# At most two scatters of the slot list in flight: a wait on one of two semaphores before each scatter

## The chip, the core and the metric

The kernel runs on one core of a Trainium2 chip. The metric is the device time of one execution in microseconds (us). Three runs of the kernel before took 1495.07, 1495.42 and 1499.51 us, so the median is 1495.42 us. The profile was taken in one execution, whose span from the first to the last instruction is 1494.3 us.

## The reference

The input is x, 2 sequences of 4096 tokens with 256 features, 8192 tokens in all. One layer is computed:

```
xn = layernorm(x)                                        # per token
s  = attention(xn)      # 16 heads of 16, 12 sampled positions per query:
     q, k, v = xn@wq.T+bq, xn@wk.T+bk, xn@wv.T+bv
     off = tanh(pw_w @ gelu(depthwise_conv3(q)) + pw_b) * 6
     positions = clip(token + linspace(-2, 2, 12) + off, 0, 4095)
     sk, sv = k, v interpolated linearly at positions
     attn = softmax(q.sk / 4 - rel_scale*|positions - token|)
     s = (sum attn*sv) @ wo.T + bo
g  = silu(mixture_of_experts(xn))   # 8 experts of hidden 512, the best 2 per token:
     scores = xn@Wr.T + br ; top 2 of scores + biases_N ; their softmax weights, renormalised
     y = sum over the 2 chosen experts e of w_e * ((silu(a_e)*b_e) @ Wl2[e] + bl2[e])
     with a_e, b_e = the halves of xn@Wl1[e] + bl1[e]
out = x + s * g
```

## The kernel before

The program has two blocks, and between them all engines meet at a barrier, so nothing of the second block starts before every engine has ended the first.

**The first block** (`front_block`) works in 16 steps of 512 tokens (`STEPS`, `GROUP` = 4 tiles of 128 tokens). It normalises x, computes v and the router's scores, then q and k, and then for each step the products of the queries with the slopes of the keys (`head_scores`, L638; ScalarE copies them out in L514, and SyncE stores them in `S_rows`, L335), the convolution (L756 to L764), the offsets (L650, L770) and the sampled positions (`positions`, L783 to L788, stored in L340). Early in this block VectorE also routes the tokens: it chooses two experts for each token and gives each of the 16384 pairs of token and choice a place in a list sorted by expert. The places are ready at L851 (`list_row`, semaphore `list_rows`).

**The slot list.** The list lies in memory off the chip (`slot_list`, 18176 entries of 4 bytes, filled beforehand with numbers of spare rows, L421). GpSimd writes the token numbers into it by 128 indirect DMAs, here called scatters (L430, `LISTED` = 128). Each takes one column of `list_row` as its addresses and one column of `token_i` as its data: 128 partitions, one number of 4 bytes each. All 128 add 16 to the same semaphore, `scattered`, as they land, and GpSimd waits only once, for 16 * 128, ahead of the load of the finished list (L450). So it issues a scatter as soon as it has issued the one before.

Among the scatters GpSimd also issues four DMAs that clear the accumulator of the expert outputs (`clear_moe`, L438, 2 MB each: after 32, 64, 96 and 120 scatters), and after the last scatter three small clears (L445 to L447). All of these DMAs go through one queue, q0, the one of GpSimd's DMAs. SyncE's are on q1.

**After the list.** VectorE waits for the loaded list at L924 and turns it into row numbers (L925, L926, tile `inv`, named token_of in the trace). This wait stands late in VectorE's own order: behind it come only the positions of the last step (L783 to L788), which SyncE then stores (L340). SyncE waits for the landing of all stores (L387 to L394), and the block ends.

**The second block** (`mix_block`) gathers the rows of xn by the list (L1156), runs the experts on 71 pairs of 128 slots (PE L1446, L1452) and adds the results back by indirect DMAs (L1175). Beside that VectorE computes the attention weights of 16 steps (L1603, L1643, L1647). At the end the weights are applied to v, projected, multiplied by the gates and stored. GpSimd's first instruction in this block is the gather L1156 by the list.

Of the kernel before, what the change touches and what calls it, by code (L numbers as in the profile page):

```python
# [64 lines left out]
LISTED = TOPK * TILES  # L65
COUNT_AT = 1
OPEN_AT = 6
ROWS_AHEAD = 4
BAND_SLOTS = 4
MOE_SLOTS = 8  # L70
# [75 lines left out]
def front_block(nc, io, dram, keep):  # L146


    with ExitStack() as ctx:
        def sb(name, shape, dt=F32):  # L150
            return ctx.enter_context(nc.sbuf_tensor(name, shape, dt))
# [4 lines left out]
        def sem(name):  # L156
            return ctx.enter_context(nc.semaphore(name))
# [53 lines left out]
        token_i = sb("token_i", [P, TOPK * TILES], I32)  # L211
# [37 lines left out]
        consts = sem("consts")  # L249
        x_loaded = [sem(f"x_loaded{u}") for u in range(ROWS_AHEAD)]  # L250
        xn_ready = sem("xn_ready")
# [35 lines left out]
        prefix_ready = sem("prefix_ready")  # L287
        list_set = sem("list_set")
        list_rows = sem("list_rows")
        scattered = sem("scattered")  # L290
        list_loaded = sem("list_loaded")

        TAIL = VROWS - TOKENS - REACH
# [15 lines left out]
        def x_in(n):  # L309
            return x_slots[n % ROWS_AHEAD].rearrange("p (a c) -> p a c", a=GROUP)  # L310

        def rows_of(n):
            return slice(n * GTOK, (n + 1) * GTOK)
# [4 lines left out]
        def _(sp):  # L318
            def load_x(n):
                sp.dma_start(x_in(n), io["x"][rows_of(n), :].rearrange("(a p) c -> p a c", p=P)).then_inc(  # L320
                    x_loaded[n % ROWS_AHEAD], 16)

            def store_xn(n):
                sp.wait_ge(xn_ready, n + 1)
                sp.dma_start(dram["xn"][rows_of(n), 0:D].rearrange("(a p) c -> p a c", p=P), xn[:, n % 2]).then_inc(
                    xn_stored[n % 2], 16)
# [11 lines left out]
            def store_pos(n):  # L338
                sp.wait_ge(pos_ready, n + 1)
                sp.dma_start(dram["pos"][rows_of(n), :].rearrange("(a p) c -> p a c", p=P), pos[:, n % 2]).then_inc(  # L340
                    pos_stored[n % 2], 16)

            def load_opening():

                sp.wait_ge(list_rows, 1)
                for u in range(SX_SLOTS):
                    sp.wait_ge(sx_stored[u], 16)
                sp.wait_ge(pos_stored[0], 16)
                for to, rows in keep["slopes_in"](0):
                    sp.dma_start(to, rows).then_inc(keep["s_loaded"], 16)  # L350
                for at, loaded in ((keep["posn"], keep["posn_loaded"]), (keep["posw"], keep["pos_loaded"])):
                    sp.dma_start(at.rearrange("p (a c) -> p a c", a=GROUP),
                                 dram["pos"][rows_of(0), :].rearrange("(a p) c -> p a c", p=P)).then_inc(loaded, 16)
# [8 lines left out]
            for n in range(STEPS):  # L362
                store_xn(n)
                if n + ROWS_AHEAD < STEPS:
                    load_x(n + ROWS_AHEAD)
                if n > 0:
# [11 lines left out]
            for n in range(STEPS):  # L378
                for a in range(GROUP):
                    store_s(n, a)  # L380
                    if a == 1 and n >= 2:
                        store_pos(n - 2)
                if n == OPEN_AT:
                    load_opening()
# [11 lines left out]
        @block.gpsimd  # L396
        def _(pool):
            nc.gpsimd.memset(zeros[:], 0.0).then_inc(zeros_set, 1)
            nc.gpsimd.memset(keep["ident"][:], 0.0).then_inc(zeros_set, 1)
            pool.wait_ge(zeros_set, 2)  # L400
            nc.gpsimd.affine_select(out=keep["ident"][:], in_=keep["ident"][:], compare_op=ALU.not_equal, fill=1.0,
                                    base=0, pattern=[[-1, P]], channel_multiplier=1).then_inc(zeros_set, 1)

            for row, rows in ((0, REACH), (REACH + TOKENS, TAIL)):
                pool.dma_start(dram["v"][row:row + rows, :], zeros[0:rows, :]).then_inc(pads_set, 16)
            nc.gpsimd.memset(ones[:], 1.0).then_inc(consts, 1)
            pool.wait_ge(consts, 1)

            nc.gpsimd.affine_select(out=below[:], in_=ones[:], compare_op=ALU.is_gt, fill=0.0, base=0,
                                    pattern=[[1, P]], channel_multiplier=-1).then_inc(consts, 1)  # L410
            nc.gpsimd.iota(rows_i[:], pattern=[[-1, EXPERTS]], base=EXPERTS, channel_multiplier=0).then_inc(consts, 1)
            nc.gpsimd.iota(base_i[:], pattern=[[P, SEQ // P]], base=0, channel_multiplier=1).then_inc(consts, 1)
            nc.gpsimd.iota(keep["tile_exp"][:], pattern=[[PAIR, SLOT_PAIRS]], base=0, channel_multiplier=0).then_inc(consts, 1)

            nc.gpsimd.iota(head_i[:], pattern=[[0, 1]], base=0, channel_multiplier=1).then_inc(consts, 1)
            nc.gpsimd.iota(spare_i[:].rearrange("p (n s) -> p n s", s=2), pattern=[[0, HIGH // 2], [P, 2]], base=0,
                           channel_multiplier=1).then_inc(consts, 1)
            nc.gpsimd.iota(token_i[:].rearrange("p (k t) -> p k t", k=TOPK), pattern=[[0, TOPK], [P, TILES]], base=-TOKENS,
                           channel_multiplier=1).then_inc(consts, 1)
            pool.wait_ge(consts, CONSTS)  # L420
            pool.dma_start(dram["list"].rearrange("(p n) o -> p (n o)", p=P), spare_i[:]).then_inc(list_set, 16)  # L421
            pool.wait_ge(gates_ready, 1)
            for q in range(4):
                some = slice(q * TILES // 4, (q + 1) * TILES // 4)
                pool.dma_start(dram["xn"][0:TOKENS].rearrange("(t p) c -> p t c", p=P)[:, some, D:], scores[:, some]).then_inc(gates_stored, 16)
            pool.wait_ge(list_set, 16)
            pool.wait_ge(list_rows, 1)
            def scatter(some):
                for c in some:
                    nc.gpsimd.indirect_dma_start(  # L430
                        out=dram["list"], out_offset=bass.IndirectOffsetOnAxis(ap=list_row[:, c:c + 1], axis=0),
                        in_=token_i[:, c:c + 1], in_offset=None).then_inc(scattered, 16)

            def clear_moe(q):

                pool.wait_ge(pos_ready, 3 * q + 3)
                some = slice(q * TILES // 4, (q + 1) * TILES // 4)
                pool.dma_start(dram["moe"][0:TOKENS].rearrange("(t p) c -> p t c", p=P)[:, some],  # L438
                               zeros[:, None, :].broadcast_to([P, TILES // 4, D])).then_inc(pads_set, 16)

            for q in range(4):
                scatter(range(q * LISTED // 4, min((q + 1) * LISTED // 4, LISTED - 8)))
                clear_moe(q)
            scatter(range(LISTED - 8, LISTED))
            pool.dma_start(dram["moe"][TOKENS:, :].rearrange("(s p) c -> p s c", p=P), zeros[:, None, :].broadcast_to([P, 2, D])).then_inc(pads_set, 16)  # L445
            pool.dma_start(dram["xn"][TOKENS:, 0:D].rearrange("(s p) c -> p s c", p=P), zeros[:, None, :].broadcast_to([P, 2, D])).then_inc(pads_set, 16)
            pool.dma_start(dram["xn"][TOKENS:, D:].rearrange("(s p) c -> p s c", p=P),  # L447
                           zeros[:, None, 0:EXPERTS].broadcast_to([P, 2, EXPERTS])).then_inc(pads_set, 16)
            pool.wait_ge(scattered, 16 * LISTED)
            pool.dma_start(spare_i[:], dram["list"].rearrange("(p n) o -> p (n o)", p=P)).then_inc(list_loaded, 16)  # L450
            pool.wait_ge(gates_stored, 16 * 4)

# [246 lines left out]
        def _(dve):  # L699
# [10 lines left out]
            def moments(n):  # L710
                u = n % 2
                dve.wait_ge(x_loaded[n % ROWS_AHEAD], 16 * (n // ROWS_AHEAD) + 16)
                for a in range(GROUP):
# [1024 lines left out]
def build(nc, io):  # L1738
# [10 lines left out]
    with ExitStack() as ctx:  # L1749
# [24 lines left out]
        with nc.sbuf_tensor("scores", [P, TILES, EXPERTS], F32) as scores, \  # L1774
                nc.sbuf_tensor("qT", [P, KC, BATCH * (SEQ + 2)], F32) as qT, \
                nc.sbuf_tensor("kT", [P, KC, TOKENS + 1 + 2 * REACH], F32) as kT:
            keep.update(scores=scores, qT=qT, kT=kT)
            front_block(nc, io, dram, keep)
# [38 lines left out]
```

## Time and profile before

| what | value |
|---|---|
| three runs: median (lowest to highest) | 1495.42 us (1495.07 to 1499.51) |
| the profiled execution: its span | 1494.3 us |
| its time beyond the span, by the median of the runs | 1.1 us |
| first block, to the barrier | 0 to 362.9 us |
| scatters of the slot list (L430) | issued from 163.6 to 339.9 us |
| second block | 362.9 to 1494.3 us |
| busy share of the span | PE 91%, VectorE 86%, ScalarE 55%, GpSimd 54% |

An engine's busy share is an average over both blocks. In the rows below, a line of the timeline gives the start, the length and the engine of an instruction or of a run of like ones, then the idle time of that engine before it and what ended it. "issue" means that nothing the profile shows was waited for. DMAs are counted on the engine that issues them, for as long as the issuing takes. When the data has landed is told by the views of landings, and by the waits.

### The profile page before, as it was taken

To read this page: it belongs to the slowest core of one execution; us is meant where nothing else is said; L and a number is where in the kernel's file an instruction comes from. 1 tells how busy PE (TensorE), PEld (TensorE's weight loads), DVE (VectorE), ACT (ScalarE), POOL (GpSimd) and SP (SyncE) were. 2 spreads that over 40 slices of the span, in tenths; PEclk is the share of its full clock that TensorE was granted. 3 is DMA by queue.
4 is the path that set the end of the run, shared out by engine and by line. 5 is a ranking of instruction groups with operands and counts; after the bars stand their busy time and mean duration, and the time that the engine had idled before them with its cause. 6 is when DMAs were issued, how large, how long until landed. Compare 5 with 4: busy or idle time off the path is not lost.

```text
span 1494.3 us, 35841 instructions
## 1 busy us (share of the span) xinstructions
PE 1361.6 (91%) x13687; PEld 1085.4 (73%) x13688; DVE 1280.2 (86%) x1504; ACT 823.8 (55%) x1889; POOL 804.3 (54%) x566
## 2 busy tenths in 40 slices
PE   5998899984799999999999998999999978797988
PEld 4864565653688888888888886887888856675766
DVE  7837655556699999999999999999999999999961
ACT  2547687864445555555555554554555436574655
POOL 1001477773587766767666877768686651311111
PEclk9999999985999999999999999999999988898999
DMA  7933366564957676768677666767777679999897
GB/s 231 352 130 101 115 203 208 166 222 158 287 122 224 170 232 161 222 161 235 183 204 214 168 179 160 214 159 201 196 190 221 133 178 232 250 218 246 217 246 148
DMA packets 203481, 293.52 MB, mean 196 GB/s; under 512 B 24833, under 2 KB 160261, under 8 KB 203123
## 3 DMA queue, kind: packets, MB, share of 16 engines
q0 software_dynamic: 65792, 146.59, 38.5%
q1 hardware_dynamic: 134915, 144.84, 33.6%
q8 instruction: 52, 0.85, 0.3%
q10 hardware_dynamic: 2672, 0.83, 0.2%
q14 instruction: 50, 0.41, 0.1%
HBM read 182.83 MB, written 117.74 MB: 201 GB/s over the span
## 4 chain that ended last, share of the span: by engine, by line
DVE 48%; DMA 8%; PE 8%; issue 6%; SPq 5%; POOL 0%; ACT 0%; POOLq 0%; DVEq 0%
DVE gslope L1647 11%; DVE parts L1643 11%; DVE parts L1603 8%; DMA band<-band_rows 7%; DVE expert_mem L1569 5%; PE pB L1480 3%; DVE parts L1615 3%; SPq L1121 2%; DVE parts L1619 2%; DVE parts L1622 1%; PE pA L1465 1%; PE pY L1490 1%; DVE gslope L1700 1%; SPq L1115 1%; DVE wgt L1708 1%
## 5 line engine op out<-in xcount | busy, mean ns | idle before, releaser
L1175 POOL DMA_INDIRECT moe_rows<-expert_mem,token_of x142 | 324.9, 2288 | 76.2 <-issue 47.9
L1446 PE MATMUL pA<-xsT,expert_mem 128*128 128x256 f32 x1136 | 264.5, 387 | 22.6 <-DMA expert_mem<-in_w_l 15.5
L1156 POOL DMA_INDIRECT expert_mem<-xn_rows,token_of x142 | 222.3, 1566 | 96.8 <-issue 74.2
L1452 PE MATMUL pY<-expert_mem 128*128 x1136 | 265.7, 387 | 0.0
L1446 PEld LDWEIGHTS pA<-xsT,expert_mem 128*128 128x128 f32 x1136 | 220.3, 195 | 55.9 <-issue 20.0
L1446 PE MATMUL pB<-xsT,expert_mem 128*128 128x256 f32 x1136 | 256.8, 379 | 0.0
L1452 PEld LDWEIGHTS pY<-expert_mem 128*128 128x128 f32 x1136 | 211.1, 191 | 42.3 <-issue 16.2
L1446 PEld LDWEIGHTS pB<-xsT,expert_mem 128*128 128x128 f32 x1136 | 215.8, 190 | 29.3
L1643 DVE SCALAR_TENSOR_TENSOR parts<-pos_pair,prob 128x768 f32<-128x768 f32 x256 | 228.0, 953 | 1.1
L1647 DVE TENSOR_REDUCE gslope<-parts 128x256 f32<-128x3072 f32 x64 | 214.7, 3354 | 2.2
L1297 ACT ACTIVATE expert_mem<-pA,b1sel 128x256 f32<-128x256 f32 x284 | 111.3, 474 | 135.3 <-issue 93.2
L1603 DVE SCALAR_TENSOR_TENSOR parts<-posT,bend 128x768 f32<-128x768 f32 x192 | 168.9, 952 | 4.1 <-ACT posT L1358 4.1
L430 POOL DMA_INDIRECT slot_list<-token_i,high_part x128 | 132.8, 1037 | 56.9 <-issue 38.7
L1306 ACT ACTIVATE expert_mem<-pB,b1sel 128x256 f32<-128x256 f32 x284 | 111.6, 477 | 92.8 <-PE pB L1446 92.8
L1315 ACT ACTIVATE expert_mem<-pY,gsel 128x256 f32<-128x256 f32 x142 | 59.7, 472 | 157.1 <-PE pY L1452 157.1
L1165 POOL DMA_DIRECT2D expert_mem<-in_w_l x71 | 68.2, 961 | 103.7 <-PE pX L1440 64.9
L618 PE MATMUL pQK<-qT,wqk 128*128 128x512 f32 x256 | 122.9, 625 | 1.0 <-ACT qT L492 0.8
L1214 POOL DMA_DIRECT2D out<-expert_mem x15 | 19.4, 1295 | 188.1 <-DVE expert_mem L1654 171.2
L1615 DVE TENSOR_TENSOR parts<-parts 128x5376 f32<-128x5376 f32 x16 | 92.2, 5763 | 0.6
L1569 DVE TENSOR_TENSOR expert_mem<-expert_mem 128x1024 f32<-128x1024 f32 x71 | 87.0, 1226 | 6.2 <-ACT expert_mem L1306 2.8
L638 PEld LDWEIGHTS pS<-kT,qm 32*64 32x64 f32 x4096 | 56.1, 139 | 45.1 <-issue 42.1
L618 PEld LDWEIGHTS pQK<-qT,wqk 128*128 128x128 f32 x256 | 48.0, 197 | 53.8 <-issue 50.2
(197 smaller groups left out, 2036.3 us busy)
## 6 DMA issues: line engine op xcount, KB each, us to landing
expert_mem<-in_w_l POOLq DMA_DIRECT2D x71, 1024.0 KB, 7.0
band<-band_rows SPq DMA_DIRECT2D x256, 96.0 KB, 5.5
S_rows<-stage SPq DMA_DIRECT2D x64, 376.0 KB
band_rows<-wgt SPq DMA_DIRECT2D x12, 1536.0 KB, 7.1
pos_pair<-pos_rows SPq DMA_DIRECT2D x28, 384.0 KB, 7.7
xn_rows<-stage SPq DMA_DIRECT2D x16, 512.0 KB, 5.4
v_rows<-stage SPq DMA_DIRECT2D x16, 512.0 KB, 4.2
moe_rows<-zeros POOLq DMA_DIRECT2D x4, 2048.0 KB
```

What stands on the lines that cost most here:

```text
L430: nc.gpsimd.indirect_dma_start(out=dram["list"], out_offset=bass.IndirectOffsetOnAxis(ap=list_row[:, c:c + 1], axis=0), in_=token_i[:, c:c ...
L618: mm = nc.tensor.matmul(pQK[:, c], wqk[:, k, first:first + P], qT[:, k, qcol(m):qcol(m) + GTOK], start=(k == 0), stop=(k == KC - 1))
L1156: nc.gpsimd.indirect_dma_start(out=xs[:, u, s], out_offset=None, in_=dram["xn"], in_offset=bass.IndirectOffsetOnAxis(ap=keep["inv"][:, 2 * ...
L1175: nc.gpsimd.indirect_dma_start(out=dram["moe"], out_offset=bass.IndirectOffsetOnAxis(ap=keep["inv"][:, 2 * n + s:2 * n + s + 1], axis=0), ...
L1306: ins = nc.scalar.activation(hid[:, h, c], pB[:, c], ACT.Identity, bias=b1sel[:, u, HC + c:HC + c + 1])
L1446: mm = nc.tensor.matmul(dst[:, c], w1[:, 1 - u, k, o * HID + c * P:o * HID + (c + 1) * P], xsT[:, k], start=(k == 0), stop=(k == KC - 1))
L1452: mm = nc.tensor.matmul(pY[:, s], hid[:, h, c, s * P:(s + 1) * P], w2[:, c, ds(e * D, D)], start=False, stop=(s == 1 and c == HC - 1))
L1569: V.tensor_tensor(hid[:, h], hid[:, h], act_a[:, h % 2], ALU.mult).then_inc(hid_ready, 1)
L1603: ins = V.scalar_tensor_tensor(in_block(parts[:, i]), in_block(posT[:].rearrange("p b q -> p (b q)")), float(i + 1 - REACH), each_in_block ...
L1615: chain.count(V.tensor_tensor(parts[:, 0:7], parts[:, 0:7], parts[:, 7:14], ALU.add))
L1643: ins = V.scalar_tensor_tensor(terms[:, i], at, float(j - REACH), prob[:], ALU.max, ALU.mult)
L1647: chain(V.tensor_reduce(G[:, :, batch * BATCHED:(batch + 1) * BATCHED].rearrange("p t j -> p j t"), terms.rearrange("p j (t r) -> p j t r" ...
```

## The change

Instead of one semaphore there are two. Scatter number c adds 16 to `scattered[c % 2]` as it lands. Ahead of scatter c, from c = 2 on, GpSimd waits until scatter c - 2, which has the same semaphore, has landed. So no more than two are in flight, and a semaphore is counted by one scatter at a time. Ahead of the load of the list GpSimd waits for both semaphores, 16 * 64 each. The order of the DMAs is as before.

```
-        scattered = sem("scattered")
+        scattered = [sem(f"scattered{u}") for u in range(SCATTERS_OPEN)]      # SCATTERS_OPEN = 2
...
             def scatter(some):
                 for c in some:
+                    if c >= SCATTERS_OPEN:
+                        pool.wait_ge(scattered[c % SCATTERS_OPEN], 16 * (c // SCATTERS_OPEN))
                     nc.gpsimd.indirect_dma_start(
                         out=dram["list"], out_offset=bass.IndirectOffsetOnAxis(ap=list_row[:, c:c + 1], axis=0),
-                        in_=token_i[:, c:c + 1], in_offset=None).then_inc(scattered, 16)
+                        in_=token_i[:, c:c + 1], in_offset=None).then_inc(scattered[c % SCATTERS_OPEN], 16)
...
-            pool.wait_ge(scattered, 16 * LISTED)
+            for u in range(SCATTERS_OPEN):
+                pool.wait_ge(scattered[u], 16 * (LISTED // SCATTERS_OPEN))
```

On GpSimd, the end of the row of DMAs before, from the third group of scatters to the end of the block (L430 is a scatter, L438 a clear of 2 MB, L450 the load of the list):

```order
L430 DMA slot_list<-token_i,high_part 18176x1 x32
L438 DMA moe_rows<-zeros 128x16x256 [waits pos_ready]
L430 DMA slot_list<-token_i,high_part 18176x1 x24
L438 DMA moe_rows<-zeros 128x16x256 [waits pos_ready]
L430 DMA slot_list<-token_i,high_part 18176x1 x8
L445 DMA moe_rows<-zeros 128x2x256
L446 DMA xn_rows<-zeros 128x2x256
L447 DMA xn_rows<-zeros 128x2x8
L450 DMA spare_i<-slot_list 128x142 [waits scattered]
```

Now, around the fourth clear (the lines are three or four further down in the changed file: L433, L441, L454), and behind the eighth scatter after it:

```order
L433 DMA slot_list<-token_i,high_part 18176x1 [waits scattered0]
L433 DMA slot_list<-token_i,high_part 18176x1 [waits scattered1]
L441 DMA moe_rows<-zeros 128x16x256 [waits pos_ready]
L433 DMA slot_list<-token_i,high_part 18176x1 [waits scattered0]
L433 DMA slot_list<-token_i,high_part 18176x1 [waits scattered1]
...
L448 DMA moe_rows<-zeros 128x2x256
L449 DMA xn_rows<-zeros 128x2x256
L450 DMA xn_rows<-zeros 128x2x8
L454 DMA spare_i<-slot_list 128x142 [waits scattered1,scattered0]
```

No instruction has moved. Each scatter but the first two now carries a wait of its own, in turn on the two semaphores, and the clears stand unchanged between them. On the other engines the rows are the same as before.

## Rows read from the trace of the kernel before

**Rows 1.** Page, part 1 and the first lines of part 2.

```profile
PE 1361.6 (91%) x13687; PEld 1085.4 (73%) x13688; DVE 1280.2 (86%) x1504; ACT 823.8 (55%) x1889; POOL 804.3 (54%) x566
POOL 1001477773587766767666877768686651311111
```

**Rows 2.** Page, part 5, the scatters: busy us, mean ns | idle before.

```profile
L430 POOL DMA_INDIRECT slot_list<-token_i,high_part x128 | 132.8, 1037 | 56.9 <-issue 38.7
```

**Rows 3.** Timeline of POOL, 150 to 500 us: start us, us, engine line op.

```profile
163.57 1.05 POOL L430 DMA_INDIRECT slot_list<-token_i,high_part  x1 [18.14 <-DVE high_part L851]
174.88 0.97 POOL L430 DMA_INDIRECT slot_list<-token_i,high_part  x1 [0.30 <-issue]
176.15 0.97 POOL L430 DMA_INDIRECT slot_list<-token_i,high_part  x1 [0.30 <-issue]
...
251.39 1.20 POOL L438 DMA_DIRECT2D moe_rows<-zeros  x1
...
338.93 0.97 POOL L430 DMA_INDIRECT slot_list<-token_i,high_part  x1 [0.30 <-issue]
...
341.39 0.74 POOL L447 DMA_DIRECT2D xn_rows<-zeros  x1
342.69 0.78 POOL L450 DMA_DIRECT2D spare_i<-slot_list  x1 [0.56 <-DMA slot_list<-token_i,high_part]
363.68 1.68 POOL L1156 DMA_INDIRECT expert_mem<-xn_rows,token_of  x1 [20.20 <-POOLq L149]
```

**Rows 4.** DMA issues by line: KB, median us to landing.

```profile
spare_i<-slot_list POOLq DMA_DIRECT2D x1, 71.0 KB, 4.0
```

**Rows 5.** Timeline of DVE, 325 to 372 us.

```profile
355.87 0.55 DVE L770 TENSOR_TENSOR off<-pOff,pw_b 128x384 f32<-128x384 f32 x1
356.34 0.23 DVE L925 CAST list_f<-spare_i 128x142 f32<-128x142 int32 x1
356.60 0.24 DVE L926 TENSOR_SCALAR token_of<-list_f 128x142 uint32<-128x142 f32 x1
357.33 0.96 DVE L783 SCALAR_TENSOR_TENSOR pos<-off,pos 128x768 f32<-128x768 f32 x1 [0.49 <-ACT off L535]
358.33 0.26 DVE L786 TENSOR_SCALAR pos<-pos 128x192 f32<-128x192 f32 x1
358.62 1.00 DVE L788 TENSOR_SCALAR pos<-pos,base 128x192 f32<-128x192 f32 x4
363.07 0.17 DVE L1564 MEMSET ones<- 3x128 bf16 x1 [3.45 <-PEq L149]
```

**Rows 6.** Waits of the SP queue, 343 to 372 us: us, times, longest.

```profile
SPq L392 <- DMA pos_rows<-pos: 2.2, 1, 2.2
```

**Rows 7.** The gathers of line L1156, whole trace: duration ns, landing us.

```profile
L1156 POOL DMA_INDIRECT expert_mem<-xn_rows,token_of x142: 945/1290/10487, 363.7 to 1170.3; - x142
DMA to landing us min/median/max: 2.8/4.8/13.8
```

**Rows 8.** DMA queues (packets, MB, share) in 251:260, 260:261 and 261:262.

```profile
q0 software_dynamic: 530, 1.91, 63.2%
q0 software_dynamic: 131, 0.17, 59.2%
q0 software_dynamic: 35, 0.02, 8.1%
```

**Rows 9.** The same view for 165 to 206 us, between start and first clear.

```profile
q1 hardware_dynamic: 4576, 5.42, 38.0%
q0 software_dynamic: 967, 0.02, 1.8%
```

**Rows 10.** Stretches: busy us of each engine, PEclk, DMA share, GB/s.

```profile
330.00:343.00 13.00, 9.56 (x207) 8.64 (x208) 3.54 (x9) 6.84 (x14) 10.30 (x12) 0.50 0.81 266
...
357.00:369.00 12.00, 0.00 (x0) 0.00 (x0) 7.85 (x15) 4.51 (x10) 4.71 (x4) 0.59 0.28 90
369.00:376.00 7.00, 4.14 (x11) 3.23 (x12) 6.96 (x9) 0.91 (x3) 6.69 (x5) 0.50 0.92 305
```

More of the change, by code:

```diff
@@ L67 @@
 OPEN_AT = 6
+SCATTERS_OPEN = 2
 ROWS_AHEAD = 4
```

## The prediction, made before the changed kernel was run

> **What bounds the kernel now.** I read the page first, then GpSimd's timeline around the scatters, then what ends the first block, then every landing that can stand in for a scatter's. The page shows PE and VectorE busy for most of the span and GpSimd for half of it, but GpSimd is at seven tenths of each slice just while it issues the scatters [rows 1]. Averages say nothing here: what counts is the barrier at 362.9 us, before which nothing of the second block starts. GpSimd's first gather comes 0.8 us behind it [rows 3].
>
> The reader is to see three things. First, the scatters run at GpSimd's own pace. They start 1.27 us apart (174.88, 176.15), 0.97 us of issuing and 0.30 us of "issue" [rows 3]; over all 128 the mean is (132.8 + 38.7) / 128 = 1.34 us, since some issues last up to 1.5 us [rows 2]; of the 56.9 us idle, 18.1 are the first one's wait for its addresses [rows 3]. They never wait for a landing. Second, the list is early: its load is issued at 342.69 and lands 4.0 us later, at 346.7 [rows 3, 4], but VectorE comes to it only at 356.34, straight out of its own work [rows 5]. So there are 9.6 us of slack, and the first block ends by the positions and their store, not by the list. Third, the tail behind the list: L925 starts at 356.34, the positions end at 359.6, SyncE waits 2.2 us for the last store, and the barrier opens at 362.9 [rows 5, 6]. That tail is 6.5 us, of which 0.5 us is a wait for ScalarE that will be over if the list is late.
>
> **What the change removes and moves.** Nothing is removed, and the order of the DMAs stays. 126 scatters gain a wait for the landing of the scatter two places ahead. Queued behind each wait on GpSimd are the next scatters, the four clears, the load of the list, and through it VectorE (L925), SyncE's last store and the barrier. So GpSimd's pace becomes two scatters in one time from issue to landing, here called a round, if that is longer than 2 x 1.34 = 2.7 us.
>
> **How long a round is.** The trace gives no landing for a scatter, but one is bracketed. The last starts at 338.93; GpSimd ends its next three DMAs at 341.39 + 0.74 = 342.13 and then still waits for a scatter, to 342.69 [rows 3]. From issue to the start of the waiting instruction is thus at least 3.2 and at most 3.76 us. The nearest likeness, the gathers of L1156, land after 2.8 us at the least and 4.8 in the median, but among much other traffic and often behind a 1 MB load [rows 7]. I take 3.5 us, inside the bracket. Bounds: 2.8 (the shortest gather, nothing for the reaction) and 5.0 (the median gather and 0.2). The scatters themselves load the queue with next to nothing, 1.8% [rows 9], so what lasts is latency, and it goes on whether SyncE's stores run (38% on q1) or have ended. 64 rounds of 3.5 us are 224 us.
>
> The Trainium skill, "DMA: Bandwidth & Descriptors", section "Anatomy of one DMA", gives every DMA of GpSimd a fixed cost of about 2.0 us, which an estimate by that page would make a round shorter than GpSimd's own pace, so that the waits would cost nothing by themselves. The bracket of at least 3.2 us contradicts it, if that cost is counted from the issue.
>
> **The clears.** The clear issued at 251.39 has moved its 2.1 MB by about 261.3: 1.91 + 0.17 MB before 261, 0.02 after it [rows 8]. That is 9.9 us from issue in q0, the queue in which the scatters stand too. Before, GpSimd went on issuing behind it and lost nothing. Now two more scatters are issued, and then it waits until the first of them has landed. In a round that starts at 0, the second scatter is issued by 2.3 us and then the clear; the queue is free at 12.2, the scatter behind lands 2.3 us later (3.5 less its issue and 0.2) and GpSimd goes on at 14.7, where it would have gone on at 7.0. That is 7.7 us for each of the four, 31 us in all. Bounds: nothing, if a scatter's landing does not depend on the clear ahead of it, and 8.3 us each with a round of 2.8 us.
>
> **The sum.** First scatter 163.6; + 224 + 31 + 1.3 (the second scatter of the last round comes that much later) = 419.9, the issue of the list's load, 77 us later than before. Landed at 423.9. VectorE's L925 goes from 356.3 to 423.9, +67.6: the first 9.6 us of the delay cost nothing because VectorE's own work covers them, the rest is on the path. Less the 0.5 us wait for ScalarE: the barrier opens 67 us later. Every wait and load of the second block hangs on the barrier, so I move it whole. The pause of PE gets longer, but its clock stood at 0.50, the lower level of 1.2 GHz, already in 330 to 343 us, and again in the first 7 us of its work in the second block after 12 us without a matmul [rows 10]; it starts cold both times, so I put nothing for it (bounds 0 and 3 us). No other engine gains: the scatters took only 1.8% of the queues' time. The profiled span becomes 1494.3 + 67 = 1561.3; with the 1.1 us by which the median of the runs lies above it, 1562.5.
>
> With both low bounds of the round (2.8) and full clears the list is 25 us late behind its slack, 1520; with 3.5 and no cost of the clears, 1532; with 5.0 throughout, 1652.
>
> **Rivals.**
>
> A. Landings are slow while SyncE stores. Until 357 us there is q1 at 38% [rows 9], and the median gather among traffic took 4.8 us [rows 7]. With rounds of 5.0 us and two clears at 6.2 us, 36 rounds are done by 357; 28 rounds of 3.5 and two clears of 7.7 remain, 113 us. The load goes out at 471.7, the barrier 119 us later: 1614. For it: the bracket was taken at a single place. Against it: that place had a clear and three stores beside it. The same page of the Trainium skill, section "Queues, rings and completion order", says that a DMA's semaphore count lands only after every earlier write of that DMA engine, across its queues, which would speak for A; no row here separates it.
>
> B. Rounds are about as short as the shortest gather, or the clears hold nothing back: 1520 to 1532. For it: 2.8 us was seen [rows 7]. Against it: 3.2 us was exceeded here, and scatter and clear stand in one queue.
>
> C. A scatter lands within two issues, 2.7 us; the waits are met on arrival and only the clears stall, four times about 7.5 us. The load goes out at 372.7, VectorE is 20 us late: 1515. Only the 0.56 us wait [rows 3] speaks against it, and that may be the reaction to a semaphore already full.
>
> D. Not slower: the semaphores fill at GpSimd's pace whatever stands ahead in the queue, clears too. Then all waits are met on arrival and the list comes as before; it may come up to 9.6 us later without any effect, and beyond that each microsecond costs one. 1495. That is also the case of a change that does not limit anything.
>
> **How the numbers follow.** Forecast (1540 to 1590) 50%, A 20%, B 17%, C 9%, D 4%. The range takes in the forecast, B, part of C and A up to 1625: 1518 to 1625. Within 0.3% (about what a measurement of this kernel can tell from no change, 4.5 us) only D ends, 3%; faster 1%, for something in D that I don't see; slower 96%.
>
> **What would show it.** In the changed profile the idle time before the scatters is put down to the landing of a scatter, not to "issue"; it is about 64 x (3.5 - 2.7) and four waits of some 8 us behind the clears. Scatters come in pairs 3.5 us apart. The load of the list goes out near 420, VectorE has one wait for it of some 60 us, PE and ScalarE are idle from about 357 to 430, and the second block lasts 1131 us as before. Pairs 5 us apart before 357 and closer after it would be A; no waits behind the clears, B; pairs 2.7 us apart, C; a barrier at 363, D. The prediction is wrong if the pace before 357 and after it differ much, or if the second block changes its length.

## The result, and the profile after

The changed kernel takes 1563.08 us in the median of 4 runs (1549.46 to 1566.25). The kernel before takes 1495.24. The ratio is 1.0426, with a 95% interval of 1.0381 to 1.047: slower by 68 us. The forecast was 1562.5. The sum came out, but its main term, one length of a round for all scatters, was too short for the first part of them and too long for the rest, and the two errors cancelled, so the total says less than it seems. Some later executions count as slow ones, over 1.5% above the fastest of their kernel (two of about 2660 us, of the kernel before and of the one with eight in flight, and five of the ten of the first run with the clears early), and every ratio is taken from the fast ones alone.

The page of the changed kernel, part 1, answers to [rows 1]. The engines' busy times have hardly changed (PE 1361.6 to 1358.5 us), only their shares of a longer span.

```profile
span 1560.8 us, 35842 instructions
PE 1358.5 (87%) x13687; PEld 1082.2 (69%) x13688; DVE 1279.0 (82%) x1504; ACT 823.2 (53%) x1889; POOL 814.7 (52%) x566
```

The scatters in part 5 of that page answer to [rows 2]. They are as long as before (132.3 us), but the idle time before them has grown from 56.9 to 133.0 us, and 88.5 us of it is now put down to the landing of an earlier scatter.

```profile
L433 POOL DMA_INDIRECT slot_list<-token_i,high_part x128 | 132.3, 1033 | 133.0 <-DMA slot_list<-token_i,high_part 88.5
```

GpSimd's timeline in the changed kernel answers to [rows 3]: start us, us, engine line, and in brackets the idle time and what ended it.

```profile
168.44 1.05 POOL L433 DMA_INDIRECT slot_list<-token_i,high_part  x1 [19.25 <-DVE high_part L855]
...
179.69 0.97 POOL L433 DMA_INDIRECT slot_list<-token_i,high_part  x1 [1.41 <-DMA slot_list<-token_i,high_part]
181.00 0.97 POOL L433 DMA_INDIRECT slot_list<-token_i,high_part  x1 [0.34 <-DMA slot_list<-token_i,high_part]
184.07 1.08 POOL L433 DMA_INDIRECT slot_list<-token_i,high_part  x1 [2.10 <-DMA slot_list<-token_i,high_part]
...
242.22 1.68 POOL L433 DMA_INDIRECT slot_list<-token_i,high_part  x1 [7.97 <-DMA slot_list<-token_i,high_part]
...
303.55 1.20 POOL L441 DMA_DIRECT2D moe_rows<-zeros  x1
305.06 1.01 POOL L433 DMA_INDIRECT slot_list<-token_i,high_part  x1 [0.30 <-issue]
306.37 1.73 POOL L433 DMA_INDIRECT slot_list<-token_i,high_part  x1 [0.31 <-issue]
316.16 0.97 POOL L433 DMA_INDIRECT slot_list<-token_i,high_part  x1 [8.06 <-DMA slot_list<-token_i,high_part]
...
365.83 1.20 POOL L441 DMA_DIRECT2D moe_rows<-zeros  x1
367.34 1.00 POOL L433 DMA_INDIRECT slot_list<-token_i,high_part  x1 [0.30 <-issue]
368.64 0.97 POOL L433 DMA_INDIRECT slot_list<-token_i,high_part  x1 [0.30 <-issue]
374.99 0.97 POOL L433 DMA_INDIRECT slot_list<-token_i,high_part  x1 [5.38 <-DMA slot_list<-token_i,high_part]
376.26 0.97 POOL L433 DMA_INDIRECT slot_list<-token_i,high_part  x1 [0.31 <-issue]
377.54 0.97 POOL L433 DMA_INDIRECT slot_list<-token_i,high_part  x1 [0.30 <-issue]
...
411.95 0.97 POOL L433 DMA_INDIRECT slot_list<-token_i,high_part  x1 [5.38 <-DMA slot_list<-token_i,high_part]
...
421.51 0.61 POOL L454 DMA_DIRECT2D spare_i<-slot_list  x1
```

The reader is to see three kinds of time. To 352 us, while the other engines work, nearly every second scatter has a wait, of 0.3 to 2.9 us (40 waits, 60.9 us, for 86 scatters); their starts are 1.97 us apart in the mean, so a round of two is 3.94 us. From 355 us on the other engines have ended and the 42 scatters left are 1.28 us apart, GpSimd's own pace: each wait is met on arrival. And behind each clear there is one long wait: 8.0 and 8.1 us in the first part, 5.4 and 5.4 us in the second.

VectorE's end of the first block answers to [rows 5]. It came to the list at 351.8 and had to wait for it for 72 us.

```profile
351.26 0.54 DVE L774 TENSOR_TENSOR off<-pOff,pw_b 128x384 f32<-128x384 f32 x1
423.76 0.24 DVE L929 CAST list_f<-spare_i 128x142 f32<-128x142 int32 x1 [71.95 <-DMA spare_i<-slot_list]
...
425.46 1.01 DVE L792 TENSOR_SCALAR pos<-pos,base 128x192 f32<-128x192 f32 x4
429.92 0.17 DVE L1568 MEMSET ones<- 3x128 bf16 x1 [3.46 <-PEq L150]
```

Stretches of the changed kernel (busy us of each engine, then PEclk, DMA share, GB/s) answer to [rows 10]. From 352 to 430 us PE, VectorE and ScalarE do next to nothing, at the lower clock level. The stretch behind it, the second block, is as long as it was: 1130.8 us here, 1131.3 before.

```profile
352.00:430.00 78.00, 0.00 (x0) 0.00 (x0) 2.68 (x9) 0.83 (x2) 46.92 (x49) 0.51 0.23 73
...
430.00:1560.80 1130.80, 1048.53 (x8691) 870.62 (x8691) 1056.67 (x893) 597.46 (x1452) 665.73 (x408) 0.96 0.77 199
```

### The profile page after: what moved, and what is told of

Its sections match the earlier page's. It is cut to its first block and busy times, and to the rows that moved or that the text cites. A ratio compares the mean times of both kernels' runs of the same rounds, so it can differ in the third digit from the quotient of the medians.

```text
span 1560.8 us, 35842 instructions
## 1 busy us (share of the span) xinstructions
PE 1358.5 (87%) x13687; PEld 1082.2 (69%) x13688; DVE 1279.0 (82%) x1504; ACT 823.2 (53%) x1889; POOL 814.7 (52%) x566
## 5 line engine op out<-in xcount | busy, mean ns | idle before, releaser
L1179 POOL DMA_INDIRECT moe_rows<-expert_mem,token_of x142 | 339.6, 2391 | 75.9 <-issue 47.1
L1160 POOL DMA_INDIRECT expert_mem<-xn_rows,token_of x142 | 218.5, 1539 | 91.0 <-issue 80.7
L433 POOL DMA_INDIRECT slot_list<-token_i,high_part x128 | 132.3, 1033 | 133.0 <-DMA slot_list<-token_i,high_part 88.5
L1444 PE MATMUL pX<-ident,expert_mem 128*128 128x128 f32 x284 | 43.1, 275 | 85.5 <-DMA expert_mem<-xn_rows,token_of 85.5
L1444 PEld LDWEIGHTS pX<-ident,expert_mem 128*128 128x128 f32 x284 | 35.7, 142 | 92.9 <-DMA expert_mem<-xn_rows,token_of 85.8
```

What stands on the lines that cost most here:

```text
L433: nc.gpsimd.indirect_dma_start(out=dram["list"], out_offset=bass.IndirectOffsetOnAxis(ap=list_row[:, c:c + 1], axis=0), in_=token_i[:, c:c ...
L1160: nc.gpsimd.indirect_dma_start(out=xs[:, u, s], out_offset=None, in_=dram["xn"], in_offset=bass.IndirectOffsetOnAxis(ap=keep["inv"][:, 2 * ...
L1179: nc.gpsimd.indirect_dma_start(out=dram["moe"], out_offset=bass.IndirectOffsetOnAxis(ap=keep["inv"][:, 2 * n + s:2 * n + s + 1], axis=0), ...
```

## The experiments

Where nothing else is said, a kernel is the changed one with one more edit, and the intervals are from the start of a scatter to the start of the next. The runs were made on several chips. On one of them the kernel before takes 1646 to 1649 us in the median, not 1495; the last section is on that. It is called the chip of 1649 here, and a time on it can only be read against that number.

### One in flight

```
-SCATTERS_OPEN = 2
+SCATTERS_OPEN = 1
```

> One scatter in flight instead of two, so that each start-to-start interval is one whole time from issue to landing. Theory T (a landing is slow only beside SyncE's stores): intervals of 3.5 to 4 us until the stores end near 352 us, 2.3 to 2.5 us after that, about 1715 us in all. Rival U (the landing takes the same 3.5 us with or without the stores, as the prediction had it, and the fast pace late in the changed kernel has another cause): 3.5 us throughout, about 1495 + 128 x 3.5 - 171 + 30 - 10 = 1790 us.

Measured: 1712.2 us, on the chip of 1649. With one in flight each interval is a landing, and GpSimd's timeline shows it directly, first beside the block's own work, then in the quiet part:

```profile
208.76 0.97 POOL L433 DMA_INDIRECT slot_list<-token_i,high_part  x1 [4.47 <-DMA slot_list<-token_i,high_part]
212.99 0.97 POOL L433 DMA_INDIRECT slot_list<-token_i,high_part  x1 [3.26 <-DMA slot_list<-token_i,high_part]
215.40 1.14 POOL L433 DMA_INDIRECT slot_list<-token_i,high_part  x1 [1.44 <-DMA slot_list<-token_i,high_part]
...
411.33 0.97 POOL L433 DMA_INDIRECT slot_list<-token_i,high_part  x1 [1.43 <-DMA slot_list<-token_i,high_part]
413.73 0.97 POOL L433 DMA_INDIRECT slot_list<-token_i,high_part  x1 [1.43 <-DMA slot_list<-token_i,high_part]
```

To 352 us the intervals are 2.39 to 7.09 us, 3.84 in the mean, without the two at the first clear. From 372 us on, after the work has ended, they are 2.40 us, one like the other, save at the clears and one of 3.4. So an undisturbed landing is 2.40 us from the issue, less than two issues of 1.28 us; beside the work it is three of them in the mean. Theory T's numbers held in the mean, though not its cause, as will be seen; the uniform 3.5 us of rival U did not.

### Four and eight in flight

```
-SCATTERS_OPEN = 2
+SCATTERS_OPEN = 4      # and 8
```

> Four in flight. Theory T: four issues take 5.1 to 5.4 us, more than most landings beside the stores (3.5 to 4), so the scatters keep GpSimd's own pace; only the four clears still stall, by 12.2 + 0.2 - 1.2 - 5.1 = 5 to 6 us beside the stores. The list's load goes out some 23 us later than before, 9.6 of them slack: about 1508 us. Rival V (landings beside the stores often take over 5 us, so four are too few as well): waits in ordinary places too, and over 1520 us.

> Eight in flight. Theory T: eight issues and the clear's own take 11.4 us, and a scatter behind a clear lands after 12.2 us, so that under 2 us is left of each clear's stall, under 8 in all, inside the slack of 9.6 us: 1495 us, the same as before. Rival W (each wait costs something by itself, or a semaphore is slow to be seen): 120 waits of 0.1 to 0.3 us, 12 to 36 us, of which the slack takes 9.6: 1498 to 1522 us.

> Eight in flight, again for a chip where before takes 1495 us. Landings were 2.4 us with nothing beside them and 3.9 us in the mean, 7 at most, beside the first block's own work, so eight issues of 1.28 us cover every one but those behind a clear, where under 2 us is left of each stall: the list is 5 to 8 us later, inside the slack of 9.6: 1495 us. Rival (each of the 120 waits costs something by itself): 1500 to 1520.

Measured: four, 1639.93 us, a ratio to the kernel before of 0.994 (0.9911 to 0.9968); eight, 1652.08 us, 1.0013 (0.9993 to 1.0032). Both were on the chip of 1649, where neither expectation can be tested. Eight in flight was run again on a chip where the kernel before takes 1497.38: 1497.61 us, a ratio of 0.9996 (0.9975 to 1.0017). In its waits GpSimd waited for no scatter at all:

```profile
POOL slot_list L433 <- issue: 38.7, 127, 0.3
...
POOL slot_list L433 <- DVE high_part L855: 19.3, 1, 19.3
```

That is the same 38.7 us of "issue" as before [rows 2]: 120 waits that are met cost nothing. So the whole loss comes from waits that are not met. No wait is left behind a clear either: the scatter that waits for the one right behind a clear starts 10.5 to 11.2 us after it at GpSimd's own pace, and in the changed kernel such a scatter had landed after 11.1 us (305.06 to 316.16), in the quiet part after 7.7 (367.34 to 374.99). Four in flight was not run where the kernel before takes 1495.

### The clears ahead of the scatters

```
-                clear_moe(q)
...
+            pool.wait_ge(r_ready, STEPS)              # once the scores of all tokens are there
+            for q in range(4):
+                pool.dma_start(dram["moe"][...][:, some], zeros[...]).then_inc(pads_set, 16)
             pool.wait_ge(gates_ready, 1)
```

> Two in flight as in the changed kernel, but the four clears are issued before the scatters, once the scores of all tokens are there (near 110 us). Theory T with the clears' stalls as read from the changed profile (8.0 and 8.1 us beside the stores, 5.4 and 5.4 after them, and 1.2 us of issuing each): the scatters go on by 18 us in the time of the stores, which is worth 11 us of scatters later, and 13 us of clears later are gone: 24 to 25 us less than the changed kernel, about 1538 us. Rival X (the time behind a clear is caught up elsewhere, so that it costs nothing): as the changed kernel, 1563 us.

> The clears ahead of the scatters, two in flight, as in the run of the same kernel whose chip gave 1649 us for the kernel before and hid the effect. Where before takes 1495: theory (scatter and clear stand in one queue; stalls of 8.0, 8.1, 5.4 and 5.4 us and 1.2 us of issuing each, as read from the changed kernel's profile) 24 to 25 us less than the changed kernel, 1538. Rival (what a clear costs is caught up elsewhere): 1563.

Measured: the first run, on the chip of 1649, gave 1632 to 1668 us, a ratio of 0.9985 (0.9943 to 1.0027), and tells nothing of the clears. The second, beside a kernel before of 1497.38, 1551.16 us, a ratio of 1.0352 (1.0314 to 1.0391). That is 12 us less than the changed kernel and half of what was expected. The waits before the scatters beside the work, from 166 to 352 us:

```profile
POOL slot_list L438 <- DMA slot_list<-token_i,high_part: 76.9, 39, 3.6
```

No wait of over 5 us stands before a scatter any more, and the two in the quiet part are gone: with two issues of 1.2 us they are 13.2 us, about all that was gained. The sum beside the work is what the changed kernel has there with its two long waits (60.9 and 16.0 us); only it is now spread over ordinary waits, 0.87 us for each of 88 scatters instead of 0.71. So by this profile the clears' stalls beside the work were caught up elsewhere: the theory was right for the quiet clears, the rival for the others. Why the ordinary waits grew was not found, and it is one profile; a second one of the changed kernel (the next experiment) has 0.69 us for each.

### The changed kernel once more, and the list at another address

```
     dram = {
+        "list": nc.dram_tensor("slot_list", [SLOTS, 1], I32).ap(),     # in the kernel before, not the changed one
...
-        "list": nc.dram_tensor("slot_list", [SLOTS, 1], I32).ap(),
```

> The changed kernel itself once more, two in flight. On the chip of the last four runs the kernel before took 1649 us, 154 more than where the change was timed, all of it in the first block: while the scatters run at GpSimd's full pace there, PE issues its matmuls many times slower. If this is such a chip: theory S (what slows PE is the pace of the scatters) expects the waits of two in flight to slow the scatters only while SyncE stores, and each stall of PE to stop the stores and so the waits, so that the time is near the kernel before's, 1630 to 1660; rival (the waits alone decide, as where the change was timed): before + 67 us. If the kernel before takes 1495 us here: 1563 by both.

> The kernel before, all scatters in flight, with only the slot list declared ahead of the other arrays in the memory off the chip, so that it lies at another address. Theory M (on the chip where before takes 1649 the small writes hit a part of memory that PE's instructions come from): the time changes by over 20 us there. Rival (the place of the list plays no part): the same as before, whichever of the two times before has here.

Measured, with a kernel before of 1498.42 us: the changed kernel 1563.98 us, a ratio of 1.0444 (1.0424 to 1.0464), the same loss again, with 6.2, 6.6, 5.4 and 5.4 us of waiting behind the clears in its profile; the kernel before with the list declared first, 1497.51 us, 1.0002 (0.9976 to 1.0028). The second had been meant for the chip of 1649 and did not come to it, so theory M was not tried.

### SyncE's stores made small, or turned into loads

```
-                sp.dma_start(bass.AP(dram["S"].tensor, ..., [[S_ROW, P], ...]), Sx[:, a])
+                sp.dma_start(bass.AP(dram["S"].tensor, ..., [[S_ROW, 1], ...]), Sx[0:1, a])       # e5: 3 KB
+                sp.dma_start(Sx[:, a], bass.AP(io["x"].tensor, ..., [[S_ROW, P], ...]))           # e6: a load
```

> Two in flight, but SyncE's stores of the slope products write 3 KB instead of 376 KB each, and the second block takes these numbers from x, so part of the result is not computed. Theory T (landings are slow only beside the stores): scatters at GpSimd's own pace of 1.27 us from the start, save beside the 384 KB stores of positions, one in 14 us; the clears stall 5.4 us each as they did after the stores; the load of the list goes out 20 to 25 us after where the kernel before has it, and the whole is about 1508 where before takes 1495. Rival Y (landings are slow beside the work of PE, VectorE and ScalarE, which ends at the same time as the stores): rounds of 3.9 us as in the changed kernel, 1563.

> Two in flight, and SyncE's 376 KB stores are turned into loads of the same shape from x into the same tile (the second block takes its numbers from x, so part of the result is not computed). Theory T1 (any traffic of that size on the 16 DMA engines slows the landings): mean start-to-start intervals of 1.9 to 2.0 us as in the changed kernel, 1560 where before takes 1495. Rival T2 (what slows them is writing to the memory off the chip, whose confirmations a scatter's semaphore waits for): intervals near 1.3 us, 1508 to 1515.

Measured, one run of each beside a kernel before of 1498.42: 1549.94 us with the small stores, 1571.28 us with the loads. The waits before the scatters, of both (us, times, longest), the small stores first:

```profile
POOL slot_list L434 <- DMA slot_list<-token_i,high_part: 63.1, 34, 6.0
```

```profile
POOL slot_list L433 <- DMA slot_list<-token_i,high_part: 97.2, 48, 7.3
```

In the changed kernel it was 88.5 us in 46. Less the long waits behind the clears, and counted only beside the block's own work, it is 0.71 us for a scatter in the changed kernel, 0.40 with the small stores and 0.89 with the loads. So theory T falls as it was put: without the stores' bytes (q1's share of the DMA engines falls from 42% to 11%) more than half of the waiting remains. The bytes have a part in it, and loads hold the landings up no less than stores, which T1 had right.

### Added work beside single scatters

One scatter in flight, and in the quiet part, before each engine's wait for the list, work of one kind after the other; for PE's small matmuls for instance:

```
+            for i in range(24):
+                ...                                    # the 64 small matmuls of head_scores
+                mm.then_inc(phase[2], 1)
+                pe.wait_ge(phase[2], i + 1)
```

> One scatter in flight, so that each start-to-start interval is a landing, and in the quiet stretch after the first block's own work, where an interval was 2.40 us, work is added that the result does not need, one kind after the other: VectorE (20 operations of 128x1024 from two tiles, 26 us), PE (56 matmuls of 128x512, 28 us), PE (24 times the 64 small matmuls of the slope products, 30 us), ScalarE (36 activations of 128x512, 29 us), SyncE (40 stores of 3 KB, 25 us), SyncE (10 stores of 376 KB, one at a time, 35 us). With the stores cut to 3 KB the scatters still waited, so the theory that only SyncE's bytes slow a landing has fallen. Theory Y1 (PE's instructions, which come from the memory off the chip): intervals of 3 us and more in the two stretches of PE, most with the small matmuls, 2.4 elsewhere. Y2 (VectorE, which keeps GpSimd from writing its descriptors): over 3 us in the first stretch alone. Y3 (the number of SyncE's DMAs): in the stretch of 3 KB stores. Y4 (ScalarE): in its stretch. Y5 (the bytes after all): only in the last. If each stretch stays near 2.4 but the last, the slowing needs several engines at once.

Measured: 1727.75 us, on the chip of 1649; what counts are the intervals in each stretch. GpSimd's timeline, two rows from each: VectorE's operations, PE's small matmuls, ScalarE's activations, the 3 KB stores, the 376 KB stores.

```profile
389.34 1.09 POOL L443 DMA_INDIRECT slot_list<-token_i,high_part  x1 [1.43 <-DMA slot_list<-token_i,high_part]
391.87 1.08 POOL L443 DMA_INDIRECT slot_list<-token_i,high_part  x1 [1.44 <-DMA slot_list<-token_i,high_part]
...
467.48 0.97 POOL L443 DMA_INDIRECT slot_list<-token_i,high_part  x1 [3.00 <-DMA slot_list<-token_i,high_part]
471.42 0.97 POOL L443 DMA_INDIRECT slot_list<-token_i,high_part  x1 [2.97 <-DMA slot_list<-token_i,high_part]
...
512.58 0.97 POOL L443 DMA_INDIRECT slot_list<-token_i,high_part  x1 [1.44 <-DMA slot_list<-token_i,high_part]
514.98 0.97 POOL L443 DMA_INDIRECT slot_list<-token_i,high_part  x1 [1.43 <-DMA slot_list<-token_i,high_part]
...
527.00 0.97 POOL L443 DMA_INDIRECT slot_list<-token_i,high_part  x1 [1.44 <-DMA slot_list<-token_i,high_part]
529.39 0.97 POOL L443 DMA_INDIRECT slot_list<-token_i,high_part  x1 [1.43 <-DMA slot_list<-token_i,high_part]
...
541.39 0.97 POOL L443 DMA_INDIRECT slot_list<-token_i,high_part  x1 [1.43 <-DMA slot_list<-token_i,high_part]
543.79 0.97 POOL L443 DMA_INDIRECT slot_list<-token_i,high_part  x1 [1.43 <-DMA slot_list<-token_i,high_part]
```

The intervals are 2.5 us beside VectorE (the issue itself is 0.1 longer, the wait for the landing is not; the first three, 3.0 to 3.3 us, follow close on the block's own last stores), 2.40 beside PE's large matmuls and ScalarE, 2.40 beside both kinds of stores but for single ones of up to 2.6. Only beside PE's small matmuls, from 457 to 497 us, they are 3.3 to 4.1 us. Of the kinds taken alone, theory Y1 is the one that holds, and for the small matmuls only. In that stretch the queue of instructions moved more than in the 54 us of large matmuls before it (packets, MB, share of 16 engines; 457 to 497 us, then 400 to 454):

```profile
q8 instruction: 10, 0.16, 1.8%
```

```profile
q8 instruction: 2, 0.03, 0.2%
```

10 packets of 16 KB in 40 us, with 1344 weight loads and as many matmuls in it: small matmuls use up instructions fast, and these come over the same 16 DMA engines. The Trainium skill, "Runtime: NRT & Kernel Launch", section "Instruction fetch mechanics", says that each engine refills its instructions in blocks of 16 KiB, 256 instructions; the 2688 of this stretch would be 10.5 blocks, and the row agrees with 10.

Is it these packets that hold a landing up, or the matmuls? The same view has the GB/s of each microsecond from 457 to 497 us, and a packet stands out in it as 16 or 17:

```profile
GB/s 0 1 0 16 1 0 0 16 1 0 0 16 1 0 0 17 0 0 0 1 16 0 0 17 0 0 0 17 0 0 16 1 0 0 16 1 0 0 17 0
```

The packets start at 460, 464, 468, 472, 477 us and so on, one in each of the long intervals (their scatters start at 460.25, 463.52, 467.48, 471.42 and 475.20). The first block's traces bear it out, when the scatters are sorted by whether a packet of an instruction queue (q8, or q14 with its 8 KB) starts within 2.4 us of a scatter's issue, those near a clear left out. With one in flight the intervals are 4.55 us with such a packet (24 of them) and 3.05 without (21). With the small stores the scatter two places on waits 0.78 us with it (43) and 0.08 without (41). There PE's small matmuls can be told from the packets: where they fill a third or more of those 2.4 us, the wait is 0.82 us with a packet (26) and 0.10 without (22). So it goes with the packets, not with the matmuls. In the changed kernel it is 1.04 against 0.45 us, and with the loads, where q1 has 50%, no difference is seen (0.96 and 1.04). No edit moved the packets alone, and one packet, at 453.5 us beside the large matmuls, held nothing up.

### Few small matmuls in the first block

```
                         for g in range(RG):
+                            if N >= 12 and (c, s, g) != (KC - 1, SUBS - 1, RG - 1):
+                                continue
```

> Two in flight as in the changed kernel, but from the 13th tile on PE issues 1 of the 64 small matmuls of the slope products (3276 of 4096 are left out, so part of the result is not computed); ScalarE copies out and SyncE stores as before. With one scatter in flight the small matmuls were the one kind of added work beside which landings rose, from 2.4 to 3.3 to 4.1 us. Theory Y1 (they lengthen the landings in the first block too): start-to-start intervals of 1.3 to 1.5 us in the mean between the clears, where the changed kernel had 1.98, few waits, the list's load 40 us earlier or more. Rival (something else in the first block, as its stores and its other work together): intervals of 1.8 to 2.0 us.

Measured: 1545.91 us beside a kernel before of 1492.54. GpSimd's group in part 5 of its page:

```profile
L433 POOL DMA_INDIRECT slot_list<-token_i,high_part x128 | 129.9, 1015 | 113.7 <-DMA slot_list<-token_i,high_part 66.1
```

66.1 us of waiting where the changed kernel had 88.5. Beside the work, and without the waits behind clears, it is 41 us for 91 scatters, 0.45 us each instead of 0.71. The load of the list goes out at 400.1, 21 us earlier, half of what Y1 expected. So Y1 explains a good third of the waiting, as the bytes of the stores do, and neither is the whole cause. It is one run of each, and leaving out matmuls left out the instruction packets too: 4 of 16 KB between 168 and 340 us instead of 28.

## Why the prediction came out

**The slack and the tail: right.** The list was late by 67.4 us at VectorE (356.3 to 423.8, forecast 423.9), and the barrier by 67, as the 9.6 us of slack and the unchanged tail demanded. Three small shifts met in it: the scatters began 4.9 us later than before, which the other profiles of these kernels also do by 2 to 5 us, the way from the first scatter to the list's load was 3 us shorter than forecast (253 against 256), and the load of the list landed in 2.2 us instead of the 4.0 of [rows 4]. Eight in flight, with its list load issued at 346.85 and VectorE at it at 356.97 without a wait, shows the slack too.

**The second block: right.** It moved whole, 1131.3 to 1130.8 us, and the longer pause of PE cost nothing.

**The round of 3.5 us throughout: the step that failed.** The prediction had said that what lasts is latency, and that "it goes on whether SyncE's stores run (38% on q1) or have ended". It does not. Beside the first block's work a round was 3.94 us, and after it the landing of 2.40 us is below the two issues of 2.55, so that GpSimd's own pace holds. The bracket of 3.2 to 3.76 us was taken at a place where the engines still worked and a clear had just been moved, and I used it for the quiet part as well. A pace that differs much before 357 us and after it was the prediction's own sign of being wrong, and it came. Rival A had the dependence on the other work right, with 5.0 us too long a round; rival C, the waits met on arrival, is what the quiet part showed. The sum over both parts came out by luck: 86 scatters at 1.97 us and 42 at 1.28 are 223 us, and the 128 at 1.75 that had been put down are 224.

The page "DMA: Bandwidth & Descriptors" of the Trainium skill, section "Anatomy of one DMA", with its fixed cost of about 2.0 us, fits the quiet landing here, 2.40 us from the start of the issue and 1.43 from its end. I had set it aside on the strength of a bracket that other work had stretched. The same page's rule in "Queues, rings and completion order", that a DMA engine's count lands only after its every earlier write, across its queues, was not borne out by the one test of stores alone: beside 376 KB stores issued one at a time the landings stayed at 2.40 us, one of 2.58 apart. In the first block, where the bytes of the stores did count, no run separates this rule from the mere sharing of the engines.

**The clears: the mechanism right, two of four too dear.** Forecast 7.7 us each, 31 in all; measured 8.0, 8.1, 5.4 and 5.4, 26.8 in all. In the changed kernel's second profile they are 6.2, 6.6, 5.4 and 5.4. The two cheap ones ran with no other traffic beside them. Moved ahead of the scatters they gave back 12 us, not 27, which is the two quiet ones with their issues; those beside the work were caught up elsewhere.

**D, not slower: excluded** by the two timings, 1.0426 and 1.0444.

**What stays open.** Taking away the bytes or the small matmuls leaves 0.40 to 0.45 us of waiting for a scatter; both together were not taken away. Without the bytes almost all that is left stands beside an instruction packet (0.78 us against 0.08), so little else seems to be needed in that kernel; but that is read from a trace and not tried. And why the bytes lengthen a landing in the first block, when the same stores alone did not, was not found.

## What to carry to other kernels

A limit on DMAs in flight costs nothing as long as the number in flight times the issue pace covers the landing; here eight times 1.28 us was enough and two was not. The landing to put in is the one beside the real work (here 3.8 us in the mean, up to 7), not a quiet one (2.4), and right behind a large DMA in the same queue it is longer still (behind 2 MB 7.7 us in the quiet part and 11 to 12 beside the work). A landing read at one place of a trace holds for the work beside that place: look for stretches of the kernel where that work differs before using it for all.

## What was not expected of the hardware

**Scatters at full pace can starve PE, on one chip.** On one chip the kernel before takes 1649.28 us in the median of 25 runs (1642.78 to 1655.66), and with eight in flight, which takes as long, the difference lies in the first block: VectorE's first instruction behind the barrier starts at 514.5 us, where the chip of 1497 has 363.7. With eight in flight there, PE waits without any releaser ahead of its small matmuls (us, times, longest, from 166 to 352 us):

```profile
PEld pS L642 <- issue: 102.2, 72, 22.6
...
PE pS L642 <- issue: 50.0, 56, 2.6
```

The same rows of the kernel with one in flight, on the same chip, 166 to 360 us:

```profile
PEld pS L642 <- issue: 40.0, 69, 3.2
...
PE pS L642 <- issue: 7.7, 15, 1.7
```

And PE's timeline on that chip, in the first run with the clears early, while the scatters go out every 1.28 us. Elsewhere 64 of these matmuls take 0.9 to 1.4 us; here a few at a time come 0.7 us apart or more, and later PE stands still for 66 us.

```profile
206.77 0.47 PE L639 MATMUL pS<-kT,qm 32*64 32x47 f32 x5 [0.97 <-issue]
207.53 0.23 PE L639 MATMUL pS<-kT,qm 32*64 32x47 f32 x1 [0.29 <-issue]
208.24 0.44 PE L639 MATMUL pS<-kT,qm 32*64 32x47 f32 x3 [0.48 <-issue]
209.68 0.45 PE L639 MATMUL pS<-kT,qm 32*64 32x47 f32 x4 [1.00 <-issue]
...
308.95 0.68 PE L639 MATMUL pS<-kT,qm 32*64 32x47 f32 x24 [66.34 <-issue]
```

It seems to lock itself in: while PE stands still nothing is stored and the scatters land quickly, so with two in flight too they keep the full pace (1.28 us in that trace, with 4 waits in all), and only one in flight, 2.4 us apart at best, lets PE go on. No 16 KB packet of q8 starts between 201.6 and 349.7 us in that trace, and the last scatter is at 339.5; whether the packets are held up or not asked for is not told by it. It is the other side of the slow landings beside instruction packets, which suggests one shared path, but that is not shown; why that chip alone was not found either. The changed kernel itself was never run there.

**A met wait is free.** 120 waits on semaphores already full added nothing to 38.7 us of "issue" between 128 scatters.
